# Keys and queries of a pair of heads in halves of one PSUM bank, split by one 512-column operation per engine

## The chip, the cores and the metric

One core of one Trainium2 chip. The time is device microseconds of one execution on that core; the median of three runs stands for a kernel.

## The reference, cut to what matters

For each of 32 batch elements (256 tokens, width 256) a transformer block: cross attention of the normalized x on a context, with a residual, then a mixture of experts (16 experts, 4 per token, plus a shared one) on the normalized result, with a residual. The change touches the attention alone:

```python
x = x + attention(layernorm(x), ctx, ctx, mask, Wq, Wk, Wv, Wo, 16)     # 16 heads of 64
# qh, kh, vh = heads of q @ Wq.T, k @ Wk.T, v @ Wv.T      (width 1024)
# scores = qh @ kh.T + mask;  probs = softmax(scores);  out = (probs @ vh) @ Wo.T
x = x + experts(layernorm(x))
```

## The kernel before, in words

**Order of the work.** `emit_attention` runs all 32 batches through one software pipeline of 512 steps; step g is head h = g mod 16 of batch g // 16. In each step TensorE does, in this order: the scores of head g (4 matmuls of 256 columns, L909, L910), the first "fill" of the step, the transposes of the probabilities of head g-3 (4, L920), a second fill, the product of probabilities and V of head g-4 (4, L933), further fills. ScalarE (L989 on) does: exponentials of head g-1 (L1001), the first half of the sum of head g-5 (L1010), the high part of the first fill, the high part of the transposed probabilities (L1019), the high parts of other fills, and the high part of a finished pair (L1028, odd steps). VectorE (L1149 on) does: masked row maxima of head g (L1161), inverse sums of head g-1 (L1136), the second half of a sum (L1171), the low part of the first fill, the low part of the transposed probabilities (L1180), the low parts of other fills, then pieces of layer norm and of the router. GpSimd scales the exponentials (L812), forms low parts of the context (L756) and of a pair's result (L761), and scatters rows. Each engine does its list in order.

**High and low parts.** A float32 product is made of three matmuls of a reduced type (fp32r), `split_products` (L82 to L87): an operand is a high part (ScalarE copies PSUM to SBUF with rounding) and a low part (VectorE subtracts the high part from the same PSUM data).

**Fills.** Everything that passes through the two PSUM banks `pj[0]` and `pj[1]` is a fill (`fill`, L835): "k" and "q" (keys and queries of a pair of heads, 6 matmuls of 256 columns each), "v" (6 of 512), "wo" (a quarter of the output product, 12 of 256), "xT" and "rT" (transposes of normalized rows, for the attention and for the router), "lg" and "lt" (router logits, once a batch, and their transpose, once in two batches), "rk" (ranks). `use` numbers them in the order of the program, and fill n takes bank n mod 2: it waits (`bank`, L829) until VectorE has counted n-1 fills done on the semaphore `s_pjfree`, that is until fill n-2 has been taken out. ScalarE waits for `s_pj`, VectorE for `s_hi`.

**Which fill in which step.** Every even step holds a "k" and the next odd one the "q" of the pair two ahead (`QK_LEAD`). Other fills, by h: wo in 14, 0, 6, 8; V in 12, 13, 4, 5; xT in 9; rT in 2; lg in 7; lt in 8 of every second batch; rk twice in the program, in 10. By this order a q fill in the odd steps 1, 3, 5, 7, 13 and 15 (and 9 in every second batch) takes the bank of the k fill of the step before.

**After a pair's q.** ScalarE's L985 and VectorE's L1128 write high and low parts into `qk_sp`, a buffer of four slots K_HI, Q_HI, K_LO, Q_LO of 256 columns. SyncE (`stack`, L642) waits for q's release and copies them by four DMAs (L650, L651) into `qk_st`, where high and low parts of one head lie on one another; the scores of that pair begin three steps after its q fill.

## Time and profile before

| | |
|---|---|
| median of 3 runs | 2112.61 us (2112.27 to 2116.42) |
| profiled execution, span on the chip | 2199.6 us |
| TensorE, matmul busy | 2073.7 us (94%) |
| TensorE, weight load busy | 1991.0 us (91%) |
| VectorE busy | 1873.9 us (85%) |
| ScalarE busy | 1681.9 us (76%) |
| GpSimd busy | 1399.5 us (64%) |
| mean granted TensorE clock | 0.989 of full |
| DMA moved | 457 MB, mean 208 GB/s |

The profiled execution is one of its own; the page gives its span and no other time for it. It is 87 us longer than the median of the runs. The attention runs from the start to about 1550 us of this span, the experts after it. Busy times are unions of instructions' intervals; a matmul's end is modelled, and successive matmuls overlap in the record (a matmul of 256 columns is shown with 0.28 us, and the next one starts 0.12 us after it), so that TensorE is shown busy also in short waits. VectorE's and ScalarE's records overlap by some 0.1 us as well.

### The profile page before, as it was taken

The page shows a single profiled execution, that of the slowest core. Times are in us where ns is not written, and L with a number is a line of the kernel's source. Part 1 is how long each engine was busy: PE and PEld are TensorE (multiplying, and loading weights), DVE is VectorE, ACT ScalarE, POOL GpSimd, SP SyncE. Part 2 cuts the span into 40 slices and gives each one's busy share as a digit, 9 for nine tenths or more (in the row PEclk, how much of TensorE's full clock was granted, in tenths as well). Part 3 has the DMA queues.
Part 4 walks back from the last instruction along what each step waited for, and adds up shares of the span by engine and source line. Part 5 has one row for each costly group of instructions (what it writes and reads, how often), then busy time and mean ns, then how long its engine had stood idle before and what let it go on. Part 6 is the DMA issues. An engine that isn't in the chain of part 4 may idle for free. (4 is left out here: it accounts for less than half of the span.)

```text
span 2199.6 us, 57839 instructions
## 1 busy us (share of the span) xinstructions
PE 2073.7 (94%) x16404; PEld 1991.0 (91%) x16404; DVE 1873.9 (85%) x6177; ACT 1681.9 (76%) x4795; POOL 1399.5 (64%) x2094
## 2 busy tenths in 40 slices
PE   7999999999999999999999999999799998898885
PEld 6999999999999998999999998999799898887884
DVE  7999999999999999999999999999864446666687
ACT  6998989889988988988888888889755554454441
POOL 4565655555555555778788877877656646656665
PEclk9999999999999999999999999999999999999997
DMA  7777877778777777866666666666678778888897
GB/s 206 183 184 182 195 182 190 179 179 191 189 185 187 183 171 175 214 181 173 176 179 173 176 168 172 171 173 178 218 263 272 266 244 283 272 285 268 271 335 243
DMA packets 262128, 457.32 MB, mean 208 GB/s; under 512 B 36544, under 2 KB 148672, under 8 KB 261824
## 3 DMA queue, kind: packets, MB, share of 16 engines
q1 hardware_dynamic: 237248, 386.48, 65.4%
q0 software_dynamic: 24576, 67.14, 9.6%
q8 instruction: 148, 2.42, 0.5%
q14 instruction: 156, 1.28, 0.2%
HBM read 141.00 MB, written 144.70 MB: 130 GB/s over the span
## 5 line engine op out<-in xcount | busy, mean ns | idle before, releaser
L812 POOL TENSOR_SCALAR E<-E,rinv 128x256 f32<-128x256 f32 x1024 | 479.6, 479 | 470.3 <-DVE rinv L1136 463.8
L1001 ACT ACTIVATE E<-E,negmax 128x256 f32<-128x256 f32 x1024 | 508.3, 501 | 3.5 <-DVE negmax L1161 3.3
L1161 DVE CUSTOM_DVE_ANT_0 E<-pS,m_in 128x256 f32<-128x256 f32 x1024 | 386.6, 414 | 18.7 <-PE pS L910 16.3
L1180 DVE TENSOR_TENSOR PT_lo<-pT,PT_hi 128x512 fp32r<-128x512 f32 x512 | 350.0, 684 | 23.8 <-ACT PT_hi L1019 20.0
L1636 POOL DMA_INDIRECT block<-expert_rows,slot x256 | 247.6, 967 | 165.9 <-remote 61.4
L1019 ACT ACTIVATE PT_hi<-pT 128x512 fp32r<-128x512 f32 x512 | 304.7, 595 | 9.1 <-PE pT L920 0.5
L920 PE MATMUL pT<-ident,E 128*128 128x128 f32 x2048 | 307.9, 273 | 0.5 <-POOL E L812 0.5
L933 PE MATMUL pV<-PT_hi,V 128*128 128x256 f32 x1024 | 286.1, 301 | 5.3 <-DVE PT_lo L1180 5.3
L909 PE MATMUL pS<-qk_st 128*128 128x256 f32 x1024 | 270.3, 286 | 9.2 <-DMA qk_st<-qk_sp 8.4
L910 PE MATMUL pS<-qk_st,qk_sp 128*128 128x256 f32 x1024 | 266.5, 282 | 0.0
L933 PE MATMUL pV<-PT_lo,V 128*128 128x256 f32 x1024 | 266.2, 282 | 0.0
L985 ACT ACTIVATE qk_sp<-pj 128x256 fp32r<-128x256 f32 x512 | 196.6, 384 | 79.8 <-PE pj L87 68.5
L920 PEld LDWEIGHTS pT<-ident,E 128*128 128x128 f32 x2048 | 237.9, 141 | 0.9 <-POOL E L812 0.8
L1128 DVE TENSOR_TENSOR qk_sp<-pj,qk_sp 128x256 fp32r<-128x256 f32 x512 | 214.5, 419 | 11.7 <-ACT qk_sp L985 3.7
L1171 DVE TENSOR_TENSOR att_sum<-pV,att_sum 64x256 f32<-64x256 f32 x512 | 211.4, 413 | 11.0 <-ACT att_sum L1010 1.8
L933 PEld LDWEIGHTS pV<-PT_hi,V 128*128 128x128 f32 x1024 | 194.4, 190 | 15.6 <-DVE PT_lo L1180 8.9
L909 PEld LDWEIGHTS pS<-qk_st 128*128 128x128 f32 x1024 | 195.0, 190 | 12.8 <-DMA qk_st<-qk_sp 12.0
L1010 ACT ACTIVATE att_sum<-pV 64x256 f32<-64x256 f32 x512 | 193.8, 379 | 16.0 <-PE pV L933 3.5
L761 POOL TENSOR_TENSOR att_lo<-att_sum,att_hi 128x256 fp32r<-128x256 f32 x256 | 190.1, 743 | 20.6 <-ACT att_hi L1028 16.3
L933 PEld LDWEIGHTS pV<-PT_lo,V 128*128 128x128 f32 x1024 | 195.1, 191 | 5.6
L1001 ACT ACTIVATION_READ_ACCUMULATOR E<-E,negmax 128x1 f32 x1024 | 196.9, 192 | 0.0
L1801 ACT ACTIVATE block<-epY 128x512 f32<-128x512 f32 x152 | 91.3, 601 | 136.7 <-PE epY L87 87.7
(268 smaller groups left out, 6941.0 us busy)
## 6 DMA issues: line engine op xcount, KB each, us to landing
qk_st<-qk_sp SPq DMA_DIRECT2D x512, 192.0 KB
qk_st<-qk_sp SPq DMA_DIRECT2D x512, 128.0 KB
sorted_rows<-qk_st SPq DMA_DIRECT2D x152, 256.0 KB, 3.5
xg<-sorted_rows SPq DMA_DIRECT2D x76, 512.0 KB
expert_rows<-block SPq DMA_DIRECT2D x76, 512.0 KB
acc<-x_plus_attention SPq DMA_DIRECT2D x35, 256.0 KB
x_in<-in_x SPq DMA_DIRECT2D x32, 256.0 KB
c_in<-in_ctxT SPq DMA_DIRECT2D x32, 256.0 KB
```

The source lines that it names most:

```text
L812: last = pool.tensor_scalar(e[:, t, :], e[:, t, :], rinv[:, r, t:t + 1], 1.0, ALU.mult, ALU.mult)
L909: pe.matmul(pS[g % 2][:, t, :], stacked[:, a, Q_HI, at], stacked[:, a, K_HI, :], start=True, stop=False)
L910: last = pe.matmul(pS[g % 2][:, t, :], plain[:, Q_HI, at], stacked[:, a, K_LO, :], start=False, stop=True)
L920: last = pe.transpose(pT[g % 2][:, k, t * P:(t + 1) * P], e[:, t, k * P:(k + 1) * P], ident[:, :])
L933: last = pe.matmul(pV[g % 2][:, 0:S], V[:, k, j, 2 * a:2 * a + 2, :], PT[g % PT_RING][part][:, k, :], start=k + part == 0, stop=k == NT - ...
L1001: last = act.activation(E[r][:, t, :], E[r][:, t, :], ACT.Exp, bias=negmax[:, r, t:t + 1], scale=-1.0, accum_out=rowsum[:, r, t:t + 1])
L1019: act.activation(PT[m % PT_RING][0][:, :, :], pT[m % 2][:, :, :], ACT.Copy).then_inc(s_pthi, 1)
L1128: last = dve.tensor_tensor(plain[:, lo, :], ps[:, 0:S], f32(plain[:, hi, :]), ALU.subtract)
L1161: last = dve.tensor_tensor_reduce(out=E[r][:, t, :], in0=pS[g % 2][:, t, :], in1=m_in.tile(b)[:, t, :], scale=-1.0, scalar=BIG, op0=ALU.ad ...
L1171: dve.tensor_tensor(att_sum[pair % 2][half(a), :], pV[n % 2][half(a), 0:S], att_sum[pair % 2][half(a), :], ALU.add).then_inc(s_sum, 1)
L1180: dve.tensor_tensor(lo[:, :, :], pT[n % 2][:, :, :], f32(hi[:, :, :]), ALU.subtract).then_inc(s_ptlo, 1)
L1636: pool.indirect_dma_start(out=cbuf[n % NCB][:, j, :], out_offset=None, in_=expert_rows[g], in_offset=bass.IndirectOffsetOnAxis(ap=shared.s ...
```

## The change

The fills get a bank from a small plan instead of by parity. "k" and "q" of a pair share one bank: k writes columns 0 to 255, q columns 256 to 511, and no other fill gets that bank between them. Any other fill, and each k, gets the bank not held that was used longest ago. k's fill waits for what was in the bank before; q's waits for no bank. k is not counted on `s_pj`, `s_hi` and `s_pjfree` any more: one ScalarE operation and one VectorE operation of 512 columns, at q's place, split both. rT moves from step 2 to 1, lg from 7 to 3, lt from 8 to 7. At the start the order k0, k1, q0, q1 becomes k0, q0, k1, q1. GpSimd's split of the context waits for the last q of a batch, where it waited for the last k.

By the plan, k of steps 2, 4, 6, 10 and 14 (and of step 8 in every second batch) follows the q of the step before in the same bank; in steps 0 and 12 (and 8 in the other batches) it takes the bank of an earlier fill.

```diff
@@ -387,7 +387,7 @@
 
     WO_STEPS = (14, H, H + 6, H + 8)
 
-    BN2_STEPS, AG2_STEP, XN2_STEP, XN_OUT_STEP, RT_STEP, LG_STEP, LT_STEP = (10, 11), 12, 13, 0, 2, 7, 8
+    BN2_STEPS, AG2_STEP, XN2_STEP, XN_OUT_STEP, RT_STEP, LG_STEP, LT_STEP = (10, 11), 12, 13, 0, 1, 3, 7
     END_STEPS = 2
 
     router = shared.router
@@ -543,12 +543,28 @@
 
         uses, number = {}, {}
 
+        bank_of, earlier = {}, {}
+        held, taken = [None, None], [None, None]
+        turn = [0, 0]
+
         def use(step, what):
-            number[what] = len(number)
+
             uses.setdefault(step, []).append(what)
+            if what[0] == "q":
+                n = bank_of["k", what[1]]
+                held[n] = None
+            else:
+                n = min((n for n in range(2) if held[n] is None), key=lambda n: turn[n])
+                earlier[what] = taken[n]
+                if what[0] == "k":
+                    held[n] = what[1]
+            bank_of[what] = n
+            turn[n] = 1 + max(turn)
+            if what[0] != "k":
+                taken[n] = number[what] = len(number)
 
         FIRST = -1
-        for what in [("xT", 0)] + [(kind, pair) for kind in "kq" for pair in range(QK_LEAD)]:
+        for what in [("xT", 0)] + [(kind, pair) for pair in range(QK_LEAD) for kind in "kq"]:
             use(FIRST, what)
         for g in range(G - H + WO_STEPS[-1] + 1):
             b, h = divmod(g, H)
@@ -748,7 +764,7 @@
 
             def split_context(b):
                 if b >= 2:
-                    pool.wait_ge(s_pj, max(number[("k", b * NP - NP - 1)], number[("v", b - 2, 2 * NT - 1)]) + 1)
+                    pool.wait_ge(s_pj, max(number[("q", b * NP - NP - 1)], number[("v", b - 2, 2 * NT - 1)]) + 1)
                 c_in.wait(pool, b)
                 hi, lo = cT[b % 2]
                 pool.tensor_copy(hi[:, :, :], c_in.tile(b)[:, :, :]).then_inc(s_chi, 1)
@@ -827,10 +843,9 @@
         @block.tensor
         def _(pe):
             def bank(what):
-                n = number[what]
-                if n >= 2:
-                    pe.wait_ge(s_pjfree, n - 1)
-                return pj[n % 2]
+                if earlier.get(what) is not None:
+                    pe.wait_ge(s_pjfree, earlier[what] + 1)
+                return pj[bank_of[what]]
 
             def fill(what):
                 kind, n = what[0], what[1]
@@ -876,7 +891,7 @@
                     pe.wait_ge(s_pjfree, number[("xT", b)] + 1)
                     for k in range(NK):
                         last = split_products(
-                            pe, ps[:, 0:S], [w[:, k, j * P:(j + 1) * P] for w in wq],
+                            pe, ps[:, S:2 * S], [w[:, k, j * P:(j + 1) * P] for w in wq],
                             [a[:, k, :] for a in xnT[b % 2]], k == 0, k == NK - 1)
                 elif kind == "k":
                     b, j = divmod(n, NP)
@@ -896,7 +911,8 @@
                         pe.wait_ge(s_attlo, n * NP + k + 1)
                         last = split_products(pe, ps[:, 0:D], [a[:, k, t * P:(t + 1) * P] for a in att],
                                               [w[:, k, :] for w in wo], k == first, k == end - 1)
-                last.then_inc(s_pj, 1)
+                if kind != "k":
+                    last.then_inc(s_pj, 1)
 
             def scores(g):
                 pair, a = divmod(g, 2)
@@ -960,10 +976,10 @@
 
             def hi_part(what):
                 kind, n = what[0], what[1]
-                if kind in ("wo", "lg", "lt", "rk"):
+                if kind in ("wo", "lg", "lt", "rk", "k"):
                     return
                 act.wait_ge(s_pj, number[what] + 1)
-                ps = pj[number[what] % 2]
+                ps = pj[bank_of[what]]
                 if kind == "xT":
                     if n >= 2:
                         act.wait_ge(s_pj, number[("q", (n - 1) * NP - 1)] + 1)
@@ -982,7 +998,7 @@
                 else:
                     if n >= QK_RING:
                         act.wait_ge(s_S, 2 * (n - QK_RING + 1))
-                    last = act.activation(qk_sp[qk_buf(n)][:, K_HI if kind == "k" else Q_HI, :], ps[:, 0:S], ACT.Copy)
+                    last = act.activation(qk_sp[qk_buf(n)][:, K_HI:Q_HI + 1, :], ps[:, :].rearrange("p (i s) -> p i s", i=2), ACT.Copy)
                 last.then_inc(s_hi, 1)
 
             start_up(weight_hi, hi_part)
@@ -1079,7 +1095,9 @@
 
             def lo_part(what):
                 kind, n = what[0], what[1]
-                ps = pj[number[what] % 2]
+                ps = pj[bank_of[what]]
+                if kind == "k":
+                    return
                 if kind == "lg":
                     dve.wait_ge(s_pj, number[what] + 1)
                     turn, at = divmod(n, SET_BATCHES)
@@ -1124,8 +1142,8 @@
                     last = dve.tensor_tensor(lo, ps[:, :].rearrange("p (j a d) -> p j a d", a=2, d=DH), f32(hi), ALU.subtract)
                 else:
                     plain = qk_sp[qk_buf(n)]
-                    hi, lo = (K_HI, K_LO) if kind == "k" else (Q_HI, Q_LO)
-                    last = dve.tensor_tensor(plain[:, lo, :], ps[:, 0:S], f32(plain[:, hi, :]), ALU.subtract)
+                    last = dve.tensor_tensor(plain[:, K_LO:Q_LO + 1, :], ps[:, :].rearrange("p (i s) -> p i s", i=2),
+                                             f32(plain[:, K_HI:Q_HI + 1, :]), ALU.subtract)
                 last.then_inc(s_pjfree, 1)
 
             def inverse_sums(g):
```

## Rows read from the trace of the kernel before

**Rows 1.** Page, first line; busy table of the attention stretch (PE, PEld, DVE, ACT, POOL).
```profile
span 2199.6 us, 57839 instructions
...
160.78:1455.98 1295.20, 1278.08 (x10156) 1231.65 (x10155) 1231.98 (x4456) 1147.50 (x3417) 861.05 (x1421) 1.00 0.73 181
```

**Rows 2.** Groups by line, same stretch: busy, mean ns | idle before.
```profile
L1019 ACT ACTIVATE PT_hi<-pT 128x512 fp32r<-128x512 f32 x433 | 257.7, 595 | 7.4
...
L1128 DVE TENSOR_TENSOR qk_sp<-pj,qk_sp 128x256 fp32r<-128x256 f32 x433 | 181.3, 419 | 6.8
...
L985 ACT ACTIVATE qk_sp<-pj 128x256 fp32r<-128x256 f32 x432 | 165.9, 384 | 62.8 <-PE pj L87 52.9 <-issue 1.1
...
L909 PEld LDWEIGHTS pS<-qk_st 128*128 128x128 f32 x865 | 164.4, 190 | 4.3 <-DMA qk_st<-qk_sp 3.6 <-issue 0.5
...
L85 PEld LDWEIGHTS pj<-xnT_hi,wq_hi 128*128 128x128 f32 x432 | 81.7, 189 | 18.3 <-DVE qk_sp L1128 15.9 <-DVE x_in L1109 1.3 <-issue 0.7
...
L85 PEld LDWEIGHTS pj<-cT_hi,wk_hi 128*128 128x128 f32 x432 | 81.4, 188 | 2.7 <-DVE qk_sp L1128 2.2
```

**Rows 3.** Timeline of TensorE, batches 10 and 11: start, us, what.
```profile
495.03 0.28 PE L909 MATMUL pS<-qk_st 128*128 128x256 f32 x1
...
497.13 0.28 PE L909 MATMUL pS<-qk_st 128*128 128x256 f32 x1
...
499.67 0.28 PE L909 MATMUL pS<-qk_st 128*128 128x256 f32 x1
...
500.47 0.39 PE L85 MATMUL pj<-xnT_hi,wq_hi 128*128 128x256 f32 x1 [0.17 <-DVE qk_sp L1128]
...
502.21 0.36 PE L909 MATMUL pS<-qk_st 128*128 128x256 f32 x1
...
505.79 0.28 PE L909 MATMUL pS<-qk_st 128*128 128x256 f32 x1
...
509.29 0.28 PE L909 MATMUL pS<-qk_st 128*128 128x256 f32 x1
...
521.48 0.28 PE L909 MATMUL pS<-qk_st 128*128 128x256 f32 x1
...
525.99 0.28 PE L909 MATMUL pS<-qk_st 128*128 128x256 f32 x1
...
542.18 0.28 PE L909 MATMUL pS<-qk_st 128*128 128x256 f32 x1
```

**Rows 4.** Timeline of VectorE, the same batches.
```profile
496.11 0.41 DVE L1161 CUSTOM_DVE_ANT_0 E<-pS,m_in 128x256 f32<-128x256 f32 x1
...
497.19 0.41 DVE L1128 TENSOR_TENSOR qk_sp<-pj,qk_sp 128x256 fp32r<-128x256 f32 x1
...
498.12 0.16 DVE L242 CAST r_topf<-r_topi 128x16 f32<-128x16 uint32 x1
...
498.65 0.42 DVE L1161 CUSTOM_DVE_ANT_0 E<-pS,m_in 128x256 f32<-128x256 f32 x1
...
499.99 0.42 DVE L1128 TENSOR_TENSOR qk_sp<-pj,qk_sp 128x256 fp32r<-128x256 f32 x1
500.33 0.68 DVE L1180 TENSOR_TENSOR PT_lo<-pT,PT_hi 128x512 fp32r<-128x512 f32 x1
500.93 0.68 DVE L1116 TENSOR_TENSOR xrT_lo<-pj,xrT_hi 128x512 fp32r<-128x512 f32 x1
...
501.86 0.41 DVE L1161 CUSTOM_DVE_ANT_0 E<-pS,m_in 128x256 f32<-128x256 f32 x1
...
515.89 0.57 DVE L1090 COPY rowcol<-pj 32x128 f32<-32x128 f32 x2
...
521.50 0.41 DVE L1128 TENSOR_TENSOR qk_sp<-pj,qk_sp 128x256 fp32r<-128x256 f32 x1
...
542.86 0.42 DVE L1161 CUSTOM_DVE_ANT_0 E<-pS,m_in 128x256 f32<-128x256 f32 x1 [0.20 <-PE pS L910]
```

**Rows 5.** Timeline of SyncE's queue, batch 10, step 10.
```profile
521.93 0.49 SPq L650 DMA_DIRECT2D qk_st<-qk_sp  x1
```

## The prediction, made blind

> **What bounds the kernel now.** I read the page's first line, then the busy table of the attention stretch, the groups of instructions by line, and last the timelines of single steps, since only these show whether a "busy" TensorE is waiting. A step (one head) begins with the first scores matmul. In 27 batches, 432 steps, 1295.20 us pass [rows 1, 2]: 47.97 us a batch of 16 steps, TensorE shown busy 1278 us, VectorE 1232, ScalarE 1148, clock at full level (1.00). What would a step cost if TensorE waited for nothing? A bare step (4 score, 6 fill, 4 transpose, 4 value matmuls) takes 497.13 - 495.03 = 2.10 us; with a V fill 509.29 - 505.79 = 3.50, so V is 1.40; with an rT fill 499.67 - 497.13 = 2.54, so rT (and the like xT) is 0.44; wo and lg, 12 and 4 matmuls of 256 columns at the spacing of about 0.12 us (2.10 over 18), are 1.43 and 0.48 [rows 3]. Sum of a batch: 16 x 2.10 + 4 x 1.43 + 4 x 1.40 + 2 x 0.44 + 0.48 = 46.3 us. So TensorE bounds attention, and 1.7 us a batch (3.5%) goes into waits; over 32 batches that is 54 us, the ceiling of what this change could return. VectorE has 45.6 us of work in the same 47.97: it is the engine that TensorE waits for, and it runs behind after short steps.
>
> Where are the waits? A q fill takes the bank that the k fill of the step before filled, and waits for its subtraction on VectorE: 15.9 us in 27 batches, 0.59 a batch; k fills 2.2 us, 0.08 [rows 2]. One case: in step 3 of batch 10 the k subtraction starts at 499.99, lasts 0.42, and the q fill starts 0.06 after its end, at 500.47, where it was due 0.48 after the step's start, at 500.15; the step takes 2.54 in place of 2.10 [rows 3, 4].
>
> **The change, part by part.** (1) **The q fill's wait goes.** q now fills the other half of k's bank, with no eviction between. Saved: 0.59 x 32 = **19 us**.
>
> (2) **Half the evictions, twice as wide.** On VectorE a 256-column subtraction holds the engine 500.33 - 499.99 = 0.34 us, a 512-column one 500.93 - 500.33 = 0.60 [rows 4]: a pair costs 0.60 where it cost 0.68, so 0.08 x 8 = 0.64 us a batch, 21 us in all. (The durations, 0.42 and 0.68, would give 0.155 a pair, but they overlap; the spacing is what the engine pays.) ScalarE: 384 twice against 595 ns [rows 2], 0.17 a pair by duration; TensorE shows no large wait on it, so I count nothing there. VectorE's saving counts only where TensorE waits for VectorE's backlog rather than for a bank: of the 1.7 us lost a batch 0.67 are bank waits, and the other 1.0 is spread over probabilities, routing work and gaps. I credit 40% of 0.64, 0.25 a batch: **8 us**; its ends are 0 and 21.
> The Trainium skill, "Perfetto Trace Analysis", section "Optimizing Scalar/DVE Operations", gives about 125 ns per VectorE operation on PSUM and advises larger operations on a saturated engine; the direction agrees with the rows, and by its figure VectorE would be freed of 8 x 0.125 x 32 = 32 us where the rows say 21.
>
> (3) **A later release, and a new wait.** k and q are both released by one operation in the odd step, and the next k fill, 0.48 into the even step, often gets the same bank: by the new order in steps 2, 4, 6, 10, 14 and, in every second batch, 8. It waits for ScalarE's and VectorE's 512 columns of the odd step. Steps 6 and 14 follow a step of 3.5 us and are safe. Step 2 follows step 1, now with rT: in batch 10 the subtraction at 497.19 would end about 497.87, the k fill is due at 495.03 + 2.54 + 0.48 = 498.05: no wait. Step 4: carry VectorE forward in batch 10. Step 1 gets 0.26 (wider) and 0.60 (rT moved in), so the row maximum of step 2 moves from 498.65 to 499.51. Step 2 lasted 501.86 - 498.65 = 3.21; less k (0.34) and rT (0.60) it is 2.27, so step 3's maximum comes at 501.78. The q subtraction follows 1.1 to 1.3 later (497.19 and 499.99 against the maxima at 496.11 and 498.65), at 502.9 to 503.1, and frees the bank at 503.6 to 503.8. The k fill is due at 499.67 + 2.10 + 0.48 (lg moved in) + 0.48 = 502.73. Wait: about 0.9 [rows 3, 4]. Batch 10 holds 0.53 of router work in step 1 (498.12 to 498.65) that only every second batch has, and it starts with backlog: its maximum of step 1 comes 496.11 - 495.03 = 1.08 after the scores, batch 11's 542.86 - 542.18 = 0.68. Without these 0.9 us the bank is free on time. So 0.45 a batch on average. Step 10: the q subtraction at 521.50 would end at 522.18, against 521.48 + 0.48 = 521.96; but lg's copies (0.57 on VectorE) and k are gone before it, and the shorter step 7 takes 0.48 back [rows 4]: 0.1 in half the batches, 0.05. Sum 0.5 x 32 = **16 us lost**.
>
> (4) **Moved steps.** rT to step 1, lg to 3, lt to 7. Each brings the same matmuls, evictions and copies; inputs are there a batch ahead; nothing of SP or POOL moves with them (the store of the normalized rows stays in step 0), and the router's choice starts no earlier. They fill short odd steps, which is counted in (3). Otherwise 0. (5) **Other fills** alternate less: V's and wo's second half waits for the first as before, one step away. 0, hidden by that step's 3.5 us; if VectorE's backlog uses it up, up to 0.3 a batch. (6) The POOL wait for q in place of k, one step later, lies 8 steps ahead of its use: 0. The start fills k0, q0, k1, q1 without eviction between: under 1 us.
>
> **Sum**: -19 - 8 + 16 = -11 us in the profiled execution: 2199.6 to about 2188. The runs are 87 us shorter than this span (2112.6); which stage that is, no row tells. I apply the same difference: 2112.6 - 11 = 2101. If the unprofiled TensorE is the faster one, VectorE bounds more, and term (2) counts whole.
>
> **Rivals.** *A, VectorE bounds* (chance 0.20, inside "faster"): the 21 us of (2) in full, and of the 19 us of (1) half stays, as the new waits fall into VectorE's backlog anyway: 2112.6 - 21 - 10 = 2082. For it: VectorE is busy 95% [rows 1]; against it: some steps run at TensorE's bare 2.10. *B, the banks cancel it* (0.17): the new k wait equals the old q wait and VectorE's freed time becomes idle: 2110 to 2115. A sibling that gives the same: the copies that stack keys and queries start 0.26 later while the steps before their use lose their waits. In batch 10 the issue at 521.93 has to land by 525.99, and steps 10 and 11 took 4.51 where 4.20 are possible [rows 3, 5]; 8 such waits, 3.6 us, are there already [rows 2]. With 0.35 a batch, 11 us: 2112. *C, slower* (0.22): the k fill in step 4 waits for q's release in every batch, with 0.9, with 0.28 in step 10 (522.18 + 0.06 - 521.96) and as much in every second step 8: 1.32 a batch against 0.59 removed, +23 us, 2136. It decides once VectorE's maximum in step 3 starts more than about 1.2 us after the scores' first matmul in both kinds of batch. For it: batch 10's arithmetic; against it: odd batches have no such backlog, and VectorE has 0.64 a batch less to do. The Trainium skill, "Perfetto Trace Analysis", section "Optimizing Tensor Performance", tells to rotate matmul groups through different banks so that one's eviction overlaps the next; here the pair and the other fills each stay in one bank for several steps, so by that rule C is the outcome. The rows above show how far: 0.5 a batch, not 1.32. That q doesn't really start without a wait is excluded by the code: it has none.
>
> **Numbers.** About 4 us (0.2%) can be told from no change. Main case 0.41 (2093 to 2107), A 0.20, B 0.17, C 0.22. Faster 0.62, same 0.16, slower 0.22. Range: down to A with part of the rest, 2079; up into C, 2123.
>
> **What would show it.** In the profile after: no idle before the xnT_hi,wq_hi fill (18.3 us on the weight loads now); idle before cT_hi,wk_hi up from 2.7 to about 14 us, in step 4 of every second batch; 216 evictions of 128x512 in place of 432 of 128x256, near 595 and 683 ns; VectorE's busy sum lower by some 20 us; a batch at 47.6 us instead of 47.97. Idle before the scores on the stacking copies above 10 us would mean B; k waits over 25 us, C; an end earlier by 30 us with VectorE at 96% busy, A.

## The result and the profile after

The changed kernel takes 2145.95 us (median of 4 runs, 2144.5 to 2147.5) where the kernel before takes 2114.52 (2112.27 to 2118.52) in the same session: ratio 1.0146, 95% interval 1.0134 to 1.0158, 31 us slower. In another session (C1 below) it was 1.0155 (1.0138 to 1.0172). Two executions far off all others (4034 us for the kernel before, 2842 us for E14) are left out of the ratios.

One thing has to be cleared away first: the 87 us between the profiled execution of before (2199.6) and its median. The kernel before took about 2115 us in some sessions and 2190 to 2201 us in others. All profiles fall into the same two groups by their time from the last scores to the end: 571 to 573 us (the change, E12 to E16) or 645 to 659 us (the kernel before, C1, E1 to E11). What makes the two groups isn't shown. The record's chip number 1 stands in both (2190.6 and 2115.3 us for the kernel before). The ratios here are all between kernels timed in the same session. The page of the changed kernel, of the first group, begins:

```profile
span 2144.7 us, 56820 instructions
## 1 busy us (share of the span) xinstructions
PE 2046.5 (95%) x16404; PEld 1978.2 (92%) x16404; DVE 1866.1 (87%) x5921; ACT 1662.6 (78%) x4539; POOL 1395.6 (65%) x2094
```

The busy table for the same 27 batches as before, and for the experts' stretch (window, length; PE, PEld, DVE, ACT, POOL; clock, DMA share, GB/s):

```profile
162.99:1479.98 1316.99, 1281.92 (x10156) 1232.51 (x10155) 1225.81 (x4240) 1126.13 (x3201) 855.91 (x1421) 1.00 0.72 178
...
1600.00:2144.00 544.00, 514.22 (x4351) 508.28 (x4349) 403.77 (x909) 310.93 (x715) 375.97 (x393) 0.98 0.91 314
```

The experts' stretch in the kernel before:

```profile
1600.00:2199.00 599.00, 520.99 (x4149) 497.08 (x4147) 376.45 (x847) 284.23 (x669) 355.69 (x368) 0.97 0.82 273
```

The 27 batches last 1316.99 us against 1295.20 [rows 1]: 48.78 a batch against 47.97, 0.81 more, though VectorE has 6 and ScalarE 21 us less to do. From the first to the last scores it is 1554.6 us against 1527.5, 27 us more. The experts' stretch has another DMA rate (314 against 273 GB/s), since the two profiles are of different groups, and can't be compared between them. The second profile of the change, C1, is of the same group as before's: it has 1559.6 us of attention, 32 more than before, and 4 us less after it, where its ratio gives 34 us. So the loss lies in the attention. Most variants below lose 1 to 9 us more by time than by this span of attention. So the times give the verdicts, and the profiles only say where.

Groups of instructions by line, same 27 batches (busy, mean ns | idle before, what ended it):

```profile
L925 PEld LDWEIGHTS pS<-qk_st 128*128 128x128 f32 x865 | 164.4, 190 | 15.0 <-DMA qk_st<-qk_sp 15.0
...
L1145 DVE TENSOR_TENSOR qk_sp<-pj,qk_sp 128x512 fp32r<-128x512 f32 x217 | 149.7, 690 | 29.2 <-ACT qk_sp L1001 27.3
...
L1001 ACT ACTIVATE qk_sp<-pj 128x512 fp32r<-128x512 f32 x216 | 129.2, 598 | 52.4 <-PE pj L87 47.8 <-issue 0.7
...
L85 PEld LDWEIGHTS pj<-xnT_hi,wq_hi 128*128 128x128 f32 x432 | 81.8, 189 | 0.0
...
L85 PEld LDWEIGHTS pj<-cT_hi,wk_hi 128*128 128x128 f32 x432 | 81.4, 188 | 30.7 <-DVE qk_sp L1145 28.5
...
L85 PEld LDWEIGHTS pj<-wv_hi,cT_hi 128*128 128x128 f32 x216 | 40.7, 188 | 12.0 <-DVE V L1142 3.6 <-DVE qk_sp L1145 1.8
```

The line of V in the kernel before, which [rows 2] leave out:

```profile
L85 PEld LDWEIGHTS pj<-wv_hi,cT_hi 128*128 128x128 f32 x216 | 40.7, 189 | 7.1 <-DVE qk_sp L1128 1.6
```

Set beside [rows 2], these account for the time. Before q 18.3 to 0.0; before k 2.7 to 30.7; before the scores 4.3 to 15.0; before V 7.1 to 12.0; before the product of probabilities (8.5 to 6.5) and lt (2.0 to 0.0) a little less. Together -18.3 + 28.0 + 10.7 + 4.9 - 2.0 - 2.0 = +21.3, of 21.8 us. The q wait went, as meant, and a larger wait came at k.

By step (each gap between matmuls of the timeline above the usual one for its kind, summed over the 27 batches, per batch), the k wait is almost all in step 4, 1.02 us: about 1.1 in the batches with router work in step 1 and 0.9 in the others. The scores wait for their stacking copies in step 12 (0.42, before 0.08) and step 4 (0.10). The q waits that went were 0.33 in step 3 and 0.29 in step 13.

**Why step 4.** Timelines of batch 10 (start, us, what, idle before). TensorE, first scores matmul of steps 1 to 4, and the k fill of step 4:

```profile
504.98 0.28 PE L925 MATMUL pS<-qk_st 128*128 128x256 f32 x1
...
507.52 0.28 PE L925 MATMUL pS<-qk_st 128*128 128x256 f32 x1
...
509.62 0.28 PE L925 MATMUL pS<-qk_st 128*128 128x256 f32 x1
...
512.68 0.39 PE L925 MATMUL pS<-qk_st 128*128 128x256 f32 x1 [0.34 <-DMA qk_st<-qk_sp]
...
513.97 0.39 PE L85 MATMUL pj<-cT_hi,wk_hi 128*128 128x256 f32 x1 [0.55 <-DVE qk_sp L1145]
```

VectorE, steps 1 to 3:

```profile
508.29 0.68 DVE L1134 TENSOR_TENSOR xrT_lo<-pj,xrT_hi 128x512 fp32r<-128x512 f32 x1
...
509.42 0.42 DVE L1179 CUSTOM_DVE_ANT_0 E<-pS,m_in 128x256 f32<-128x256 f32 x1
...
510.30 0.43 DVE L1189 TENSOR_TENSOR att_sum<-pV,att_sum 64x256 f32<-64x256 f32 x1
...
511.70 0.41 DVE L1179 CUSTOM_DVE_ANT_0 E<-pS,m_in 128x256 f32<-128x256 f32 x1
...
513.23 0.69 DVE L1145 TENSOR_TENSOR qk_sp<-pj,qk_sp 128x512 fp32r<-128x512 f32 x1 [0.21 <-ACT qk_sp L1001]
```

ScalarE, steps 2 and 3:

```profile
509.42 0.60 ACT L1035 ACTIVATE PT_hi<-pT 128x512 fp32r<-128x512 f32 x1
510.76 0.42 ACT L1044 ACTIVATE att_hi<-att_sum 128x256 fp32r<-128x256 f32 x1 [0.74 <-DVE att_sum L1189]
511.09 0.49 ACT L1017 ACTIVATE E<-E,negmax 128x256 f32<-128x256 f32 x1
...
512.19 0.38 ACT L1026 ACTIVATE att_sum<-pV 64x256 f32<-64x256 f32 x1
512.59 0.60 ACT L1001 ACTIVATE qk_sp<-pj 128x512 fp32r<-128x512 f32 x1
```

Read backwards. The k fill of step 4 starts 0.05 after VectorE's subtraction ends (513.92). VectorE had stood idle 0.21 ahead of that, waiting for ScalarE's high parts (512.59). ScalarE was that late because its exponentials of step 3 began at 511.09, 1.47 after the scores, and ahead of them its queue stood still 0.74 at `att_hi` (L1044), until VectorE's half sum of step 2 was done. That sum was late (510.30) because step 1 had rT's low part (508.29) to do. So the link reads VectorE, ScalarE, VectorE, TensorE, each in its own order; E13 tests its part through ScalarE. (The description of the kernel before, and the expectation of E12, place `att_hi` in odd steps; the trace has it in the even ones: it is the head g-5 that is odd.)

The waits between the engines tell the same over the window (engine, line, waited for: us, times, longest). After:

```profile
ACT att_hi L1044 <- DVE att_sum L1189: 54.3, 115, 1.4
...
PEld pj L85 <- DVE qk_sp L1145: 30.3, 41, 1.5
DVE qk_sp L1145 <- ACT qk_sp L1001: 27.3, 144, 0.2
```

Before:

```profile
ACT att_hi L1028 <- DVE att_sum L1171: 28.4, 64, 1.4
```

Averaged over 27 batches, in us after the first scores matmul of step 3 (read from the timelines of these kernels and of experiments told below):

| step 3 | exponentials start | q high part (ScalarE) | low part (VectorE) ends |
|---|---|---|---|
| before | 0.79 | 2.31 to 2.69 | 3.55 |
| changed | 1.20 | 2.71 to 3.31 | 4.05 |
| changed, rT, lg and lt at their old steps (E1) | 0.77 | 2.28 to 2.88 | 3.71 |
| changed, lg and lt at their old steps (E3) | 1.21 | 2.72 to 3.32 | 4.06 |
| changed, split ahead of half sum (E5) | 1.20 | 2.19 to 2.77 | 3.53 |
| changed, `att_hi` on GpSimd (E13) | 0.44 | 1.96 to 2.56 | 3.60 |

The changed kernel's step 3 lasts 2.67 on average, so its bank comes free 1.38 into step 4, where k is due at 0.48. Of the 0.50 by which the release is later than before, 0.16 are there with the old steps (E1) and 0.35 come with rT in step 1 (E3).

### The profile page after: what moved, and what is told of

The parts are those of the page before. It is cut to its first block and busy times, and to the rows that moved or that the text cites. A ratio compares the mean times of both kernels' runs of the same rounds, so it can differ in the third digit from the quotient of the medians.

```text
span 2144.7 us, 56820 instructions
## 1 busy us (share of the span) xinstructions
PE 2046.5 (95%) x16404; PEld 1978.2 (92%) x16404; DVE 1866.1 (87%) x5921; ACT 1662.6 (78%) x4539; POOL 1395.6 (65%) x2094
## 5 line engine op out<-in xcount | busy, mean ns | idle before, releaser
L1145 DVE TENSOR_TENSOR qk_sp<-pj,qk_sp 128x512 fp32r<-128x512 f32 x256 | 176.6, 690 | 39.2 <-ACT qk_sp L1001 37.2
L1001 ACT ACTIVATE qk_sp<-pj 128x512 fp32r<-128x512 f32 x256 | 153.0, 598 | 66.8 <-PE pj L87 61.6
L926 PEld LDWEIGHTS pS<-qk_st,qk_sp 128*128 128x128 f32 x1024 | 195.0, 190 | 0.1
```

The lines of the kernel that those rows point to most:

```text
L926: last = pe.matmul(pS[g % 2][:, t, :], plain[:, Q_HI, at], stacked[:, a, K_LO, :], start=False, stop=True)
```

## The experiments

Theory T after the result: the common release comes too late for the k fill in step 4, because of the rearranged steps and the later eviction. Rivals: the moved steps alone do it; the shared bank alone does it; the width of the operations does it. E1 to E4 have 4 to 5 runs each, the later ones 4 to 12.

One thing goes with lg's place and must be kept apart from the work that lg brings: which bank the k fill of step 4 gets. With lg in step 3 it is the bank of step 3's q, in the change and, by parity, in E2 as well. With lg in step 7 (the kernel before, E1, E3) it is the bank of the rT fill, and the V fill of step 4 gets the q's. This follows from the order in `use`.

**E1: the change with rT, lg and lt at their old steps.**
```diff
-    BN2_STEPS, AG2_STEP, XN2_STEP, XN_OUT_STEP, RT_STEP, LG_STEP, LT_STEP = (10, 11), 12, 13, 0, 1, 3, 7
+    BN2_STEPS, AG2_STEP, XN2_STEP, XN_OUT_STEP, RT_STEP, LG_STEP, LT_STEP = (10, 11), 12, 13, 0, 2, 7, 8
```


> The change with rT, lg and lt back in steps 2, 7 and 8; the bank plan and the 512-column evictions stay. By the plan the k fill of step 4 then takes the bank of rT (step 2), not that of step 3's q. Theory P (the loss is the bank: k of step 4 filled into the bank that step 3's q has just filled, 1.0 us a batch): the wait before cT_hi,wk_hi in step 4 goes, 32 x 1.0 = 33 us less than the change, 2113 or a little under. Theory W (the 512-column evictions are late everywhere, and with them bank release and stacking copies): most of the loss stays, 2130 or more.

Measured: 1.0041 (1.0026 to 1.0056). Attention 1535.3 us. In its groups by line the k wait is nearly gone; the scores and V wait instead:

```profile
L925 PEld LDWEIGHTS pS<-qk_st 128*128 128x128 f32 x865 | 164.4, 190 | 15.4 <-DMA qk_st<-qk_sp 14.6 <-issue 0.4
...
L85 PEld LDWEIGHTS pj<-cT_hi,wk_hi 128*128 128x128 f32 x432 | 81.5, 189 | 4.6 <-DVE qk_sp L1145 4.5
...
L85 PEld LDWEIGHTS pj<-wv_hi,cT_hi 128*128 128x128 f32 x216 | 40.7, 188 | 16.6 <-DVE qk_sp L1145 7.1 <-DVE V L1142 4.1
```

That is about 2123 us on the first scale, between the ranges of the two theories. The shared bank and the wide operations, with the rest of the plan, cost 0.4%, though they take away the q wait and 216 operations on each engine. The moved steps, with the bank that they give step 4's k, cost the other 1.0%.

**E2: the kernel before with rT, lg and lt moved, nothing else.**
```diff
-    BN2_STEPS, AG2_STEP, XN2_STEP, XN_OUT_STEP, RT_STEP, LG_STEP, LT_STEP = (10, 11), 12, 13, 0, 2, 7, 8
+    BN2_STEPS, AG2_STEP, XN2_STEP, XN_OUT_STEP, RT_STEP, LG_STEP, LT_STEP = (10, 11), 12, 13, 0, 1, 3, 7
```


> The kernel before with only the three steps moved (rT 1, lg 3, lt 7), banks by parity, 256-column evictions. Theory P: the moved steps alone are harmless, 2105 to 2118. Theory S (rT in step 1 puts ScalarE behind for steps 2 and 3, so the release in step 3 is late whatever the banks are): slower than before by 10 to 25 us, 2125 to 2140, with the wait in steps 3 and 4 grown.

Measured: 1.0069 (1.0045 to 1.0093). Its weight-load groups:

```profile
L85 PEld LDWEIGHTS pj<-xnT_hi,wq_hi 128*128 128x128 f32 x432 | 81.7, 189 | 6.9 <-DVE qk_sp L1128 6.7
L85 PEld LDWEIGHTS pj<-cT_hi,wk_hi 128*128 128x128 f32 x432 | 81.5, 189 | 17.1 <-DVE qk_sp L1128 17.0
```

Theory S's range. The move takes away most of the q wait (18.3 to 6.9) and makes a k wait in step 4 (0.54 a batch): there, too, this k fill now takes the bank of step 3's q, which VectorE frees 0.87 into step 4. It costs 0.7% alone and 1.0% with the shared bank. By the span of attention it costs only 6 of its 15 us; 3.5 more stand after the last scores, and the rest isn't located.

**E3: the change with rT moved, lg and lt at their old steps.**
```diff
-    BN2_STEPS, AG2_STEP, XN2_STEP, XN_OUT_STEP, RT_STEP, LG_STEP, LT_STEP = (10, 11), 12, 13, 0, 1, 3, 7
+    BN2_STEPS, AG2_STEP, XN2_STEP, XN_OUT_STEP, RT_STEP, LG_STEP, LT_STEP = (10, 11), 12, 13, 0, 1, 7, 8
```


> The change with rT in step 1 but lg and lt back in 7 and 8. The plan then gives step 4's k the other bank (rT's, three steps old), while ScalarE has rT's copy in step 1 as in the change. Theory P: as fast as with all steps back, about 2113. Theory S: ScalarE's backlog in step 3 is still there and shows up at the next fill or at the scores, 2130 or more.

Measured: 1.0072 (1.0051 to 1.0093), attention 1540.1. rT's move costs 0.3% over E1, that of lg and lt another 0.7 to 0.8%. The idle before k is 5.0 us, against 30.7. Yet the release in step 3 is as late as in the change (4.06 and 4.05, table above): rT in step 1 makes it late. What is gone is the k fill's need for it, since this k now takes rT's bank; the V fill takes the q's, and the idle before V is 18.7 us in place of 12.0, before the product of probabilities 11.5 in place of 6.5. So the wait of k needs both the late release and lg in step 3. How much of lg's 0.7 to 0.8% is that bank and how much its work in step 3, no run separates.

**E4: the change with two 256-column operations on each engine, both at q's place.**
```diff
-                    last = act.activation(qk_sp[qk_buf(n)][:, K_HI:Q_HI + 1, :], ps[:, :].rearrange("p (i s) -> p i s", i=2), ACT.Copy)
+                    for i in range(2):
+                        last = act.activation(qk_sp[qk_buf(n)][:, K_HI + i, :], ps[:, i * S:(i + 1) * S], ACT.Copy)
...
-                    last = dve.tensor_tensor(plain[:, K_LO:Q_LO + 1, :], ps[:, :].rearrange("p (i s) -> p i s", i=2),
-                                             f32(plain[:, K_HI:Q_HI + 1, :]), ALU.subtract)
+                    for i in range(2):
+                        last = dve.tensor_tensor(plain[:, K_LO + i, :], ps[:, i * S:(i + 1) * S],
+                                                 f32(plain[:, K_HI + i, :]), ALU.subtract)
```


> The change with each 512-column eviction of a pair as two of 256 columns, at the same place; banks and steps as in the change. The difference is what width alone is worth. By the spacing of the records (0.34 against 0.30 on VectorE, 0.28 against 0.24 on ScalarE per 256 columns) each engine pays 0.084 us more a pair. Theory P, release chain only: step 4's bank comes free up to 0.17 us later, 5 us a run, 2151. If VectorE's busy time counts throughout: 8 x 0.084 x 32 = 21 us more, 2167.

Measured: 1.0226 (1.0202 to 1.0251); attention 1574.7 against 1554.6 to 1559.6 for the change itself. Groups by line:

```profile
L85 PEld LDWEIGHTS pj<-cT_hi,wk_hi 128*128 128x128 f32 x432 | 81.3, 188 | 44.0 <-DVE qk_sp L1147 42.4
...
L1147 DVE TENSOR_TENSOR qk_sp<-pj,qk_sp 128x256 fp32r<-128x256 f32 x433 | 163.4, 418 | 40.1 <-ACT qk_sp L1002 36.1 <-issue 0.5
```

So the wide operation is worth 15 to 20 us *in this layout*, 11 to 13 of them directly at the k fill (44.0 against 30.7, and 32.9 in C1). Beside two narrow operations at the same place, width isn't at fault. A variant that splits k in its own step and keeps the shared bank wasn't run, so the cost of the common release isn't measured apart from that of the bank.

**C1: the change once more, beside E5 to E7** (no edit).

> The change itself again, beside the kernel before on the chip of this call, as the measure for the three that follow. On the first chip it was 31 us slower than before. Expert work differs between chips (from the last scores to the end 654 us in one profile, 572 in the other), attention does not (the scores from first to last: 1527 us before, 1555 after): if that is the whole of it, the difference is again about 30 us, whatever the two absolute times.

Measured: 1.0155 (1.0138 to 1.0172); attention 1559.6, idle before k 32.9, before the scores 15.7. The waits repeat.

**E5: the change, with the pair's split ahead of the half sum where a wait follows.** ScalarE's high part in steps 3, 5, 11, 13; VectorE's low part in 3, 5, 9, 11, 13.
```diff
+                todo = uses.get(g, ())
+                if g % H in (3, 5, 11, 13):
+                    for what in todo[:1]:
+                        hi_part(what)
                 n = g - SUM_LAG
...
-                todo = uses.get(g, ())
-                for what in todo[:1]:
-                    hi_part(what)
+                if g % H not in (3, 5, 11, 13):
+                    for what in todo[:1]:
+                        hi_part(what)
```


> The change, with the pair's eviction taken before the half sums: on ScalarE in steps 3, 5, 11 and 13 (there it is behind, and the q fill is ready before it), on VectorE in those and step 9. Nothing is added or left out. Theory R (what TensorE waits for is the release of the pair's bank and, through it, the stacking copy): in step 3 the high parts start at about 2.3 in place of 2.71 us after the scores, the release comes 0.4 earlier, the wait of step 4's k falls from 1.0 to about 0.6 a batch, the scores of step 12 wait 0.2 less: 15 to 22 us under the change. Theory V (VectorE and ScalarE are short of time as a whole, and the release is only where it shows): the order on them moves nothing, within 5 us of the change.

Measured: 1.0136 (1.0119 to 1.0153). That is 6 us below C1, its neighbour in the same session, and all four times of E5 lie under all four of C1: a small gain, near theory V and far from theory R. Weight-load groups:

```profile
L85 PEld LDWEIGHTS pj<-cT_hi,wk_hi 128*128 128x128 f32 x432 | 81.5, 189 | 16.8 <-DVE qk_sp L1149 14.8
...
L85 PEld LDWEIGHTS pj<-wv_hi,cT_hi 128*128 128x128 f32 x216 | 40.9, 189 | 24.1 <-DVE rowcol L1112 8.3 <-DVE V L1146 7.8 <-issue 2.2
```

The release in step 3 comes 0.52 earlier and half the k wait goes (30.7 in the change and 32.9 in C1, to 16.8). The V fills take most of it over (12.0 and 12.3, to 24.1; step 4 alone 0.39 a batch). Moving the release forward in the queue moved most of the wait to the next bank.

**E6: E5 with the steps at their old places** (E1's edit and E5's).

> As the one before, and rT, lg and lt back in steps 2, 7, 8 (the bank plan with no q-k reuse in step 4, which came out 8 us over before in the attention). Theory R: the waits left there were the scores of step 12 (0.46 a batch), V in 4, 12 and 13 (0.4) and k in 10 (0.1); released 0.15 to 0.4 earlier these shrink by half: 10 to 15 us less than with the steps back alone, a little faster than before (ratio 0.995 to 1.000). Theory V: ratio 1.004 as with the steps back alone.

Measured: 1.0054 (1.0038 to 1.0071), against 1.0041 for E1. Idle before k 0.9, before V 19.2, before the scores 10.8: the same exchange, and not the gain that theory R asked for.

**E7: the kernel before, with its splits ahead of the half sum** (ScalarE in steps 2, 3, 4, 5, 11, 12, 13; VectorE also in 9; the edit is E5's with these steps).

> The kernel before, with the first fill's eviction taken before the half sums in the steps where ScalarE runs behind (2 to 5 and 11 to 13; on VectorE also 9). Theory R: the q waits of steps 3 and 13 (0.33 and 0.29 a batch) go for the most part, as the k they wait for is out 0.4 earlier: 10 to 18 us faster than before (ratio 0.992 to 0.995). Theory V: no difference from before.

Measured: 0.9996 (0.9986 to 1.0006), nothing. Weight-load groups:

```profile
L85 PEld LDWEIGHTS pj<-xnT_hi,wq_hi 128*128 128x128 f32 x432 | 81.8, 189 | 4.5 <-DVE qk_sp L1132 2.7 <-DVE x_in L1113 1.0 <-issue 0.5
...
L85 PEld LDWEIGHTS pj<-wv_hi,cT_hi 128*128 128x128 f32 x216 | 40.7, 188 | 18.4 <-DVE V L1128 10.5 <-issue 2.1 <-DVE qk_sp L1132 0.5
```

This removes 14 of the 18.3 us of q wait from the kernel before, without any of the change, and gains nothing: V's idle goes from 7.1 to 18.4. The 19 us that the prediction booked for this wait couldn't be had by earlier releases alone.

**E8 and E11: less VectorE work, in the kernel before and in the change.** The layer-norm statistics are taken over half of the columns, so a part of the computation is left out. 126 instructions in the attention's loop become 417 - 283 = 0.134 us shorter, 17 us in all.
```diff
-                dve.bn_stats(st6[:, t, :], x_in.tile(b)[:, t, :]).then_inc(s_bn, 1)
+                dve.bn_stats(st6[:, t, :], x_in.tile(b)[:, t, 0:D // 2]).then_inc(s_bn, 1)
...
-                dve.bn_stats(st62[:, t, :], x_in.tile(b)[:, t, :]).then_inc(s_bn2, 1)
+                dve.bn_stats(st62[:, t, :], x_in.tile(b)[:, t, 0:D // 2]).then_inc(s_bn2, 1)
```


> The kernel before with the four layer-norm statistics of a batch taken over half the columns, 128 of 256 (part of the computation left out). Nothing that TensorE waits for by name is touched; VectorE gets 4 x about 0.13 = 0.53 us a batch back, 17 us in all, much as the change gives it. Theory V (TensorE's waits are VectorE's and ScalarE's backlog, wherever they show): 8 to 17 us faster, ratio 0.992 to 0.996. Theory R (single releases decide, free time on VectorE is worth nothing): under 4 us, ratio 0.998 to 1.000.

> The same omission in the change. If VectorE's backlog makes the waits of step 4 and 12 there: 10 to 17 us under the change, ratio to before 1.008 to 1.010. If it is ScalarE's, whose exponentials come at 1.20 us in step 3 and which has the wide copies and rT's in step 1: under 5 us, ratio 1.013 to 1.016.

Measured: E8 0.9983 (0.9975 to 0.9992), 3.7 us of 17, 22% (10 to 32% by the interval). E11 1.0141 (1.0126 to 1.0156), the change's own ratio; idle before k 30.0. Busy table of E8:

```profile
158.93:1448.13 1289.20, 1275.64 (x10156) 1230.86 (x10155) 1221.68 (x4456) 1145.55 (x3417) 860.38 (x1421) 1.00 0.73 182
```

VectorE's busy sum is 10 us below that of before, and the 27 batches 6 us shorter, which would be 41% of their 14.5; but two profiles of one kernel (the change and C1) differ by 5 us in these batches, so the rate by time stands. VectorE's time counts only where TensorE waits for it. These statistics lie in certain steps, so the rate holds for those, and in the changed kernel E11 shows hardly any. E11 leaves the exponentials of step 3 at 1.21 and the release at 4.07.

**E10 and E9: the fourth quarter of wo from step 8 to 10** (step 10 is a step with no such work; E10 in the kernel before, E9 in E1).
```diff
-    WO_STEPS = (14, H, H + 6, H + 8)
+    WO_STEPS = (14, H, H + 6, H + 10)
```


> The kernel before with the fourth quarter of the output product in step 10 in place of 8, so that three short steps in a row (9, 10, 11) are broken by a long one. Theory V: backlog is what short steps in a row build up, waits of steps 10 to 13 (0.7 us a batch) go by more than half, those of 9 may grow: 8 to 15 us faster, ratio 0.993 to 0.996. Theory R: q of step 11 now waits for k of 10 in its bank, that of 13 for k of 12 as before: within 4 us.

> The change with rT, lg and lt back and that quarter in step 10. The scores of step 12, which waited 0.46 us a batch for the stacking copies, have 1.4 us more between q of step 9 and their use: that wait goes. Theory V and R both: 10 to 15 us under the steps-back kernel (ratio 1.004 there), 0.997 to 0.999. A ratio of 0.993 or less would mean that the shared bank and the wide evictions do pay once the steps fit them.

Measured: E10 1.0044 (1.0031 to 1.0057), E9 1.0076 (1.0063 to 1.0089). In E10 the waits of steps 10 to 13 go (idle before the scores 0.7 in place of 4.3) and come back in step 9, as q's wait, 0.37 a batch, and xT's, 0.39. In E9, xT's wait in step 9 is 0.65 and k's in step 10 0.52. Moving this fill was a loss in both, against all expectations. The likely reason, not tested by itself: step 8 is now short, so xT and q come sooner than VectorE is done for them. For xT it isn't a bank: in batch 10 of E10 it waits 0.80 for the normalized rows (L1065).

**E12 to E14: is it ScalarE, held by VectorE?** `att_hi`, on which ScalarE stands still 54.3 us (28.4 before), goes to GpSimd, ahead of its own `att_lo`. E12 is that in the kernel before, E13 in the change, E14 in E1.
```diff
@ GpSimd
+                b, j = divmod(pair, NP)
+                pool.wait_ge(s_sum, 2 * pair + 2)
+                if b and j % (NP // 2) == 0:
+                    pool.wait_ge(s_pj, number[("wo", b - 1, NT - 1 if j == 0 else WO_LAST)] + 1)
+                pool.tensor_copy(att[0][:, j, :], att_sum[pair % 2][:, :]).then_inc(s_atthi, 1)
...
@ ScalarE
...
-                    act.activation(att[0][:, j, :], att_sum[pair % 2][:, :], ACT.Copy).then_inc(s_atthi, 1)
```


> The kernel before with the high part of a finished pair (L1028, 0.31 us of ScalarE in each odd step, 2.5 us a batch) formed by GpSimd ahead of its low part. VectorE freed by 17 us gave only 4 us; theory A is that ScalarE's place in the odd steps is what TensorE's waits hang on: its exponentials start at 0.77 to 0.79 us in step 3 in every kernel with rT in step 2, however light VectorE is. A: the lag of steps 3, 4, 11 to 13 falls by 0.3 or more, 10 to 20 us faster, ratio 0.991 to 0.995. Not A: within 4 us, or slower if GpSimd's later scaling holds up the transposes.

> The same in the change. A: the exponentials of step 3 start near 0.8 in place of 1.20, release of the pair's bank 0.3 to 0.4 earlier, the wait of step 4's k from 1.0 to 0.6 or less; 12 to 20 us under the change, ratio to before 1.006 to 1.010. Not A: ratio 1.013 or more.

> The same with rT, lg and lt back in 2, 7, 8. A: 10 to 15 us under the steps-back kernel (1.004), ratio 0.997 to 0.999, the wait of step 12's scores on the stacking copies the largest that is left (0.3 a batch or more). If it comes out under the kernel before with the same edit, shared bank and wide evictions pay once ScalarE has room; if over, they don't even then.

Measured: E12 1.0033 (1.0021 to 1.0044), E13 1.0057 (1.0043 to 1.0071), E14 1.0020 (1.0011 to 1.0030). Busy table and weight-load groups of E13:

```profile
163.87:1463.70 1299.83, 1277.08 (x10157) 1231.53 (x10155) 1220.39 (x4240) 1049.25 (x2985) 946.41 (x1637) 1.00 0.73 180
```

```profile
L929 PEld LDWEIGHTS pS<-qk_st 128*128 128x128 f32 x865 | 164.5, 190 | 13.5 <-DMA qk_st<-qk_sp 13.2
...
L85 PEld LDWEIGHTS pj<-cT_hi,wk_hi 128*128 128x128 f32 x432 | 81.4, 188 | 20.2 <-DVE qk_sp L1142 18.3
```

The same edit gives the change 0.9% (19 us, and 19.0 by the span of attention, 1554.6 to 1535.6) and costs the kernel before 0.3%. The exponentials of step 3 start 0.44 after the scores in place of 1.20, the bank is free 0.45 earlier, and the idle before k falls by 10.5. The edit takes back 19 of the 31 us, inside theory A's 12 to 20. That supports the link through ScalarE, but doesn't prove it alone: part of the gain can be the 77 us of work that ScalarE no longer has, and the two are not separated. Why E12 loses 0.3% is open.

Set beside E12, which has the same edit, E13 is 0.3% slower (2127.2 against 2121.7 us) and E14 is equal (2121.4). So with `att_hi` on GpSimd in both, the change costs 0.3% in place of 1.5%, and the shared bank with the old steps nothing that can be told. E14 missed its range (0.997 to 0.999): the shared bank does no harm then, but doesn't pay.

**E15: E14 with VectorE's low part ahead of its half sum in steps 3, 9, 11; E16: the kernel before with the same in 2, 9, 12.** These were tries at a version faster than both.

> The best form of the shared bank so far (three steps back, the finished pair's high part on GpSimd, ratio 1.002), with VectorE taking the pair's low parts before the half sum in steps 3, 9 and 11. There ScalarE is done at 2.0 to 2.4 us and the half sum ends at 2.3 to 3.0, so the release can come 0.2 to 0.4 us earlier. If what is left is the latency of the release (scores of step 12, V of step 4): 5 to 10 us less, ratio 0.997 to 0.999, at or under the kernel before. If the waits only move to the V fills, as they did before: ratio 1.001 to 1.003.

> The kernel before with the fill's low part before the half sum on VectorE alone, and only where a q fill waits for it: steps 2 and 12 (k, for q of 3 and 13) and 9. ScalarE's order is as before. If the q waits of steps 3 and 13 (0.6 us a batch together) can be had for nothing so: 8 to 15 us faster, ratio 0.993 to 0.996. If they move on, as with the order changed on both engines: ratio 0.998 to 1.001.

Measured: E15 1.0030 (1.0018 to 1.0041), E16 0.9998 (0.9989 to 1.0007). Weight-load groups of E16:

```profile
L85 PEld LDWEIGHTS pj<-xnT_hi,wq_hi 128*128 128x128 f32 x432 | 81.7, 189 | 6.9 <-DVE qk_sp L1128 5.2 <-DVE x_in L1109 1.3 <-issue 0.2
...
L85 PEld LDWEIGHTS pj<-wv_hi,cT_hi 128*128 128x128 f32 x216 | 40.6, 188 | 17.0 <-DVE V L1124 6.8 <-DVE qk_sp L1128 3.8
```

Again 11 us of q wait gone, V's idle up by 10. E15 takes k's idle down to 1.4 us and is no faster than E14. No version that does the whole computation was faster than the kernel before: the lowest are E7 (0.9996) and E16 (0.9998).

## Why the prediction was wrong

It said 2101 (2079 to 2123, faster 0.62); measured 2146. The likeliest case had the right waits in view and gave them wrong sizes, and put one term at nothing, the moved steps. Of the rivals, C (slower, 0.22) describes what happened, and 31 us is even more than its 23.

**Step (1), the q wait goes, 19 us: true as a record, wrong as a gain.** Idle before q went from 18.3 to 0.0 in 27 batches. But E7 and E16 take 14 and 11 us of that wait away by another way and gain nothing, because V's fills wait longer by about as much. The step added up the wait as if nothing stood behind it. These runs take the wait away by earlier evictions; that the shared bank's own way brought nothing either is an inference from them.

**Step (2), wider operations, 8 us.** The operations came out as forecast: 690 and 598 ns at 216 to 217 of them, and E4 shows that they beat two narrow ones by 15 to 20 us in the same layout. The 40% credit had no row; E8 gave 22% (10 to 32%) and E11 next to nothing. "TensorE shows no large wait on ScalarE, so I count nothing there" failed: the wait was one link further back, on VectorE for ScalarE (27.3 us before the split) and on ScalarE for VectorE (54.3). VectorE's busy sum fell by 6 us, not some 20, in a window 22 us longer, though the records of the pair's subtractions alone fell from 181.3 to 149.7 us.

**Step (3), the new k wait, 0.5 a batch: the step that failed most.** 1.14 a batch (30.7 / 27), 1.02 of it in step 4. For batch 10 the estimate was near (0.9; batches with router work wait about 1.1). Wrong was "without these 0.9 us the bank is free on time" for the others, which wait about 0.9. The step passed the whole 0.9 us (router work and backlog of step 1) on to step 3. But there the maxima of the two kinds of batch start only 0.32 apart (2.04 and 1.72 after the scores), and the releases 0.38 (4.25 and 3.87). In the kernel before it is 0.32 as well (2.24 and 1.92), so the trace of the kernel before already had it. The carrying forward was of VectorE alone: it let the subtraction follow the maximum by 1.1 to 1.3, where it follows by 1.5, since it now waits for ScalarE, whose exponentials in step 3 are 0.4 later with rT in step 1 (E3). Rival C had put its deciding point at a maximum 1.2 us after the scores in step 3. On average it starts 1.87 after them (2.07 before), and the prediction's own rows have it at 501.86 - 499.67 = 2.19 in batch 10 [rows 3, 4].

The rule of the Trainium skill, "Perfetto Trace Analysis", section "Optimizing Tensor Performance", was weighed there with "0.5 a batch, not 1.32". It tells to rotate matmul groups through different banks; the runs side with it in direction: the shared bank with the old steps (E1) costs 0.4%, though nothing that can be told once `att_hi` is on GpSimd (E14 beside E12).

**Step (4), moved steps, "otherwise 0": wrong.** E2: +0.7% with no other edit; E1 to the change: +1.0%; E3: rT about 0.3%, lg and lt 0.7 to 0.8%. This is the largest part of the loss. Filling short odd steps looked free by TensorE's count. But in the kernel before VectorE's maxima start 1.44, 0.99, 1.37 and 2.07 us after the scores in steps 0 to 3: it catches up only in step 1, and that is where rT went. And lg in step 3 is what gives step 4's k the bank of step 3's q, in the shared layout and by parity alike; the step named only TensorE's and the evictions' work.

**Steps (5) and (6): small as said, but for V.** Idle before V +4.9 us, inside the "up to 0.3 a batch". The start: first scores at 18.3 us instead of 18.0.

**Rival B's sibling** (the stacking copies, up to 0.35 a batch) came in full and in addition: idle before the scores 4.3 to 15.0 us, 0.40 a batch, mostly in step 12. Before, step 12 had a median slack of 0.82 us between landing and scores, after 0.17. The copies for it are issued 0.27 later after the start of q's step (2.73 and 3.00), as the wider operation would have it, and take longer from issue to landing (3.53 and 4.15); why they take longer is open. No run changed the copies alone. With the steps back (E1) the wait stays, 15.4: it belongs to the shared bank and its wide release, not to the moved steps. It was priced as a rival to the k wait; the two don't exclude each other.

The signs the prediction asked for decided well: "k waits over 25 us, C" (30.7) and "idle before the scores above 10 us, B" (15.0). In short, step (3) booked 0.5 us a batch for k where 1.14 came, step (4) booked nothing where the moved steps cost 0.7 to 1.0%, and step (1) booked 19 us that came back as other waits. That the sum was wrong is shown; how the 31 us divide between the late release, the bank of step 4's k and lg's work is not.

## What to carry to other kernels

- A wait for a bank can be the visible end of the evicting engines' backlog. Before booking it as a gain, name which fill waits next: here E7 and E16 removed 14 and 11 us of one wait and gained nothing, and E5 removed 16 and gained 6.
- A fill that is moved also changes the banks of the fills behind it. Write the order down, fill by fill, and see which bank each one waits for.
- When two fills share a bank and one release, look at the first fill after it. It has only its own step's lead (here 0.48 us) against the whole chain of two evictions, and it waits if the engines lag more than the short steps allow. Carry all in-order queues forward, not the busiest one: an operation that waits for another engine (`att_hi`, 54.3 us here) holds everything behind it.
- A step that is short on TensorE isn't free room; the other engines may be using it to catch up. Test such a move by itself, as in E2.

## What the runs showed of the hardware

One kernel ran at two speeds in different sessions, and nearly all of the difference lay in the part with the most DMA traffic. The changed kernel has 1554.6 us of attention and 571.7 from its last scores to the end in one profile (timed at 2146), 1559.6 and 649.9 in the other (C1, timed at 2227). From 1600 us on all DMA engines together move 314 GB/s in the first and 274 in the second; in the attention it is 178 and 177. The cause isn't shown. A difference of a profile from the median of other runs can be just that, and is not to be put down to the profiling.

A 256-column subtraction on VectorE is 418 to 419 ns in every variant and a 512-column one 690, so the double width costs 1.65 times one and not 2; on ScalarE 384 and 598, 1.56 times. The Trainium skill, "Perfetto Trace Analysis", section "Optimizing Scalar/DVE Operations", gives an overhead of about 125 ns per VectorE operation on PSUM as the engine's busy time, and says that the profiled latency of an instruction is about twice that. What one operation less saved here is smaller by either measure: 2 x 0.34 - 0.60 = 0.08 us by spacing [rows 4], against 125 ns, and 2 x 419 - 690 = 148 ns by duration, against twice that.
